# Attention scores of the first 128 queries as three fp32r matmuls of 128 columns, with the FFN weights kept in the raw weight buffers

## What is computed

```
h = _L0_tok_ref(x, log_dt, log_w_real, w_imag, 512)            # (8, 256, 512)
h = h + attn(_layernorm(h), w_q, w_k, w_v, w_o)
h = h + ffn(_layernorm(h), ...)

# attn: 16 query heads, 4 kv heads, head width 128, 256 tokens per image
q, k = q*cos + rotate_half(q)*sin, k*cos + rotate_half(k)*sin
scores = einsum('bhqd,bhkd->bhqk', q, k) / sqrt(128)           # causal, window 256
out = einsum('bhqk,bhkd->bhqd', softmax(scores + bias), v) @ w_o
```

## Time and profile before

| what | value |
|---|---|
| median of 3 runs | 848.62 us (846.26 to 848.85) |
| the profiled execution, its own time | 845.99 us |
| span of the profile | 844.2 us |
| PE busy | 742.8 us, 88% of the span |
| PEld / DVE / ACT / POOL busy | 682.9 / 582.4 / 450.1 / 449.7 us |
| mean granted TensorE clock | 0.968 of full |
| DMA | 26.46 MB in the whole span |

### The profile page before, as it was taken

The page is one execution under the profiler, slowest core; times in us unless marked ns, Lnnn a source line. Parts: engine busy times, 40 slices in busy tenths (PEclk is TensorE's granted clock), DMA queues, the critical chain, the costliest instruction groups (busy, mean ns, idle before and its releaser), DMA issues.

```text
span 844.2 us, 19648 instructions
## 1 busy us (share of the span) xinstructions
PE 742.8 (88%) x6932; PEld 682.9 (81%) x6932; DVE 582.4 (69%) x1618; ACT 450.1 (53%) x1243; POOL 449.7 (53%) x669
## 2 busy tenths in 40 slices
PE   0038748899999999999999999999999999999985
PEld 0027747799999999999999999999999998998772
DVE  7957966677776655565666666566665677777877
ACT  5524415556655756555556565555756645554420
POOL 0198943644454747444547574444746565556522
PEclk9998978899999999999999999999999999999996
DMA  9004370100001102000001020000000000000002
GB/s 199 6 2 89 76 256 25 43 1 1 0 1 38 51 1 76 0 0 0 0 1 50 1 76 0 0 0 1 26 26 1 2 1 26 25 25 25 1 26 75
DMA packets 30533, 26.46 MB, mean 31 GB/s; under 512 B 22476, under 2 KB 22860, under 8 KB 30228
## 3 DMA queue, kind: packets, MB, share of 16 engines
q1 hardware_dynamic: 30484, 25.84, 10.9%
HBM read 17.44 MB, written 8.39 MB: 31 GB/s over the span
## 4 chain that ended last, share of the span: by engine, by line
PE 77%; DVE 11%; POOL 4%; issue 3%; ACT 2%; DMA 1%; DVEq 0%; SPq 0%; ACTq 0%; POOLq 0%
PE bank L1188 17%; PE bank L1190 17%; PE bank L1189 17%; PE bank_pair L1188 4%; PE bank_pair L1190 4%; PE bank_pair L1189 4%; POOL w_lo L421 2%; PE bank L1319 2%; PE bank_pair L1319 2%; DVE bank_pair L878 2%; PE bank_pair L1329 1%; PE bank L1329 1%; PE bank L1333 1%; PE bank L1200 1%; PE bank L1273 1%
## 5 line engine op out<-in xcount | busy, mean ns | idle before, releaser
L1188 PE MATMUL bank<-xt_hi,w_hi 128*128 (+1 forms) x768 | 217.5, 283 | 2.3 <-DVE xt_lo L949 1.5
L1189 PE MATMUL bank<-xt_hi,w_lo 128*128 (+1 forms) x768 | 215.1, 280 | 0.0
L1190 PE MATMUL bank<-xt_lo,w_hi 128*128 (+1 forms) x768 | 215.1, 280 | 0.0
L957 DVE TENSOR_TENSOR kq<-bank,cst 128x512 f32<-128x512 f32 (+1 forms) x96 | 57.9, 603 | 142.0 <-ACT swap L669 106.8
L489 POOL TENSOR_TENSOR swap<-swap,cst 128x512 f32<-128x512 f32 (+1 forms) x96 | 105.7, 1103 | 83.2 <-ACT swap L669 80.0
L1188 PEld LDWEIGHTS bank<-xt_hi,w_hi 128*128 128x128 f32 x768 | 145.2, 189 | 3.3 <-issue 1.9
L1190 PEld LDWEIGHTS bank<-xt_lo,w_hi 128*128 128x128 f32 x768 | 145.0, 189 | 0.0
L1189 PEld LDWEIGHTS bank<-xt_hi,w_lo 128*128 128x128 f32 x768 | 144.8, 188 | 0.0
L347 POOL TENSOR_TENSOR spare<-cst 1x1 f32<-1x1 f32 x87 | 16.6, 191 | 226.1 <-DVE rinv L1091 141.1
L709 ACT ACTIVATE sm<-sm,mx 128x128 f32<-128x128 f32 (+1 forms) x256 | 113.6, 445 | 21.6 <-DVE mx L1081 21.5
L668 ACT ACTIVATE swap<-bank 64x512 f32<-64x512 f32 (+1 forms) x96 | 50.2, 523 | 126.6 <-PE bank L1190 123.8
(11 more groups left out here) (245 smaller groups left out, 1900.3 us busy)
## 6 DMA issues: line engine op xcount, KB each, us to landing
mixed<-st SPq DMA_DIRECT2D x32, 128.0 KB, 2.0
out<-x SPq DMA_DIRECT2D x16, 256.0 KB, 2.1
raw<-in_w_qkv SPq DMA_DIRECT2D x8, 384.0 KB, 3.5
raw<-in_w_o SPq DMA_DIRECT2D x10, 256.0 KB, 2.7
x<-mixed SPq DMA_DIRECT2D x2, 1280.0 KB, 10.3
norm_mem<-in_w_qkv SPq DMA_DIRECT2D x6, 384.0 KB, 3.7
x<-mixed SPq DMA_DIRECT2D x3, 512.0 KB, 5.2
norm_mem<-in_w_o SPq DMA_DIRECT2D x6, 256.0 KB, 2.8
```

The costliest lines, as they stand in the source:

```text
L957: v.tensor_tensor(view(kq), src, table(cosT), ALU.mult).then_inc(kq_cos, 1)
L1188: mmul(dst, lh, rh, start=start and k == 0, stop=False, skip_group_check=True)
L1189: mmul(dst, ll, rh, start=False, stop=False, skip_group_check=True)
L1190: last = mmul(dst, lh, rl, start=False, stop=stop and k == n - 1, skip_group_check=True)
```

## The change

The fp32 matmul of each head's query tile 0 becomes a `split_product` of three fp32r matmuls of 128 columns. For this `kq_hi` and `kq_lo` hold q for all 256 tokens, so that two of the three parts that ACT, POOL (and once DVE) make grow from 128x256 to 128x512. Both tiles get longer. `fw` and `dw` no longer have memory of their own: they become views of `raw`, and SP loads them there once the last raw weights have been split. For the table `pw` the gate weights are loaded near the start into `fw_early`, which lies in memory that the first stage gives back.

```diff
@@ rope_view
     h = slice(2 * j - 1, 2 * j + 1)
-    return (..., (lambda t: t[:, h, P:S]),
-            (lambda t: t[:, j * S:(j + 1) * S].rearrange("p (h q) -> p h q", h=2)))
+    return (..., (lambda t: t[:, h, :]),
+            (lambda t: t[:, (2 * j - 1) * S:(2 * j + 1) * S].rearrange("p (h q) -> p h q", h=2)))
@@ memory
-        fw = sb("fw", [P, KC, FC])
-        dw = sb("dw", [MC, D])
+        spent = raw[:].rearrange("p r c -> p (r c)")
+        fw = spent[:, 0:KC * FC].rearrange("p (k f) -> p k f", k=KC)
+        dw = spent[0:MC, KC * FC:KC * FC + D]
+        fw_early = sb("fw_early", [P, KC, FC], F32, mixer)
-        kh = sb("kq_hi", [P, S + QH * P], F32R)
-        kl = sb("kq_lo", [P, S + QH * P], F32R)
+        kh = sb("kq_hi", [P, (1 + QH) * S], F32R)
+        kl = sb("kq_lo", [P, (1 + QH) * S], F32R)
@@ SP
-            sp.dma_start(fw[:], w_gate).then_inc(gate_in, 16)
-            sp.dma_start(dw[:], w_upd).then_inc(gate_in, 16)
+            sp.dma_start(fw_early[:], w_gate).then_inc(gate_in, 16)
...
             for n in range(KC + 2, NCK * NG):
                 load_raw(n)
+            wait_split(sp, NCK * NG - 1)
+            sp.dma_start(fw, w_gate).then_inc(ffn_in, 16)
+            sp.dma_start(dw, w_upd).then_inc(ffn_in, 16)
             with sp.Fori(0, NB) as bb:
@@ DVE, table pw
-            dve.wait_ge(gate_in, 80)
+            dve.wait_ge(gate_in, 64)
@@ PE, scores
                     bank = banks[3 + j]
-                    mmul(bank[:, 0:P], kq[:, 1 + j, 0:P], kq[:, 0, 0:P], start=True, stop=True, skip_group_check=True)
-                    qs = slice(S + j * P, S + (j + 1) * P)
-                    split_product(bank[:, P:3 * P], [(kh[:, qs], kl[:, qs], kh[:, 0:S], kl[:, 0:S])]).then_inc(s_ready, 1)
+                    for t, cols in ((0, slice(0, P)), (1, slice(P, 3 * P))):
+                        qs = slice((1 + j) * S + t * P, (1 + j) * S + (t + 1) * P)
+                        ks = slice(0, (t + 1) * P)
+                        last = split_product(bank[:, cols], [(kh[:, qs], kl[:, qs], kh[:, ks], kl[:, ks])])
+                    last.then_inc(s_ready, 1)
@@ PE, step, last group
+                        if at == 2:
+                            pe.wait_ge(ffn_in, 32)
                         gate_product(b - 2)
```

More of the change, by code:

```diff
@@ L87, in rope_view @@
     h = slice(2 * j - 1, 2 * j + 1)
-    return ((lambda t: t[:, h, :]), (lambda c: c.unsqueeze(1).to_broadcast([P, 2, S])), (lambda t: t[:, h, P:S]),
-            (lambda t: t[:, j * S:(j + 1) * S].rearrange("p (h q) -> p h q", h=2)))
+    return ((lambda t: t[:, h, :]), (lambda c: c.unsqueeze(1).to_broadcast([P, 2, S])), (lambda t: t[:, h, :]),
+            (lambda t: t[:, (2 * j - 1) * S:(2 * j + 1) * S].rearrange("p (h q) -> p h q", h=2)))
 RUNS = [
@@ L306, in raw_turn @@
             return sum(raw_slot(m) == raw_slot(n) for m in range(n + 1))
-        cst_in, par_in, mix_in, gate_in = sem("cst_in"), sem("par_in"), sem("mix_in"), sem("gate_in")
+        cst_in, par_in, mix_in, gate_in, ffn_in = sem("cst_in"), sem("par_in"), sem("mix_in"), sem("gate_in"), sem("ffn_in")
         raw_in = [sem(f"raw_in{k}") for k in range(6)]
@@ L906, in _ @@
                         sum_b(s, it * 2 + s)
-            dve.wait_ge(gate_in, 80)
+            dve.wait_ge(gate_in, 64)
             for k in range(KC):
-                sel = fw[:, k, 0:NE * SE].rearrange("p (n s) -> p n s", n=NE)
-                mean = fw[:, k, NE * SE:NE * SE + NE]
-                upd = fw[:, k, NE * SE + NE:FC].rearrange("p (n h) -> p n h", n=NE)
+                sel = fw_early[:, k, 0:NE * SE].rearrange("p (n s) -> p n s", n=NE)
+                mean = fw_early[:, k, NE * SE:NE * SE + NE]
+                upd = fw_early[:, k, NE * SE + NE:FC].rearrange("p (n h) -> p n h", n=NE)
                 row = pw[:, k, 0:FC]
@@ L1285, in update_product @@
                 for t in range(TT):
-                    mmul(banks[first_bank + t][:], mt[:, t * P:(t + 1) * P], dw[:], start=True, stop=True).then_inc(d_ready, 1)
+                    mmul(banks[first_bank + t][:], mt[:, t * P:(t + 1) * P], dw, start=True, stop=True).then_inc(d_ready, 1)
             def out_product(i):
```

## The result

| | before | after |
|---|---|---|
| median of 4 runs each, side by side | 848.29 us (846.26 to 848.85) | 856.16 us (856.01 to 856.38) |
| the profiled execution, its own time | 845.99 us | 856.01 us |
| span of the profile | 844.2 us | 854.2 us |

The ratio is 1.0097, 95% interval 1.0080 to 1.0115: slower, as forecast, but by 7.9 us (10.0 between the two profiled executions) where 15.8 were forecast.

What follows compares the result with a forecast made beforehand. PE's unbroken stream was taken to bound the kernel. Scores +13.9, lower clock +0.4, changes of group +1.2 and start +0.3 gave +15.8 us (15.0 to 17.9), so 864 us, range 861 to 867.

Steps and rivals of the forecast that it cites:

- Three short fp32r matmuls for one fp32 product, +13.9 us, and +0.4 at the lower clock: PE's scores: 0.112 us more per head over 124 heads; the first iteration's four heads, at 1.2 GHz, add 0.4.
- x: Price of one 128-column fp32r matmul on PE: taken as 0.112 us, bounded by 0.110 and 0.118.
- The FFN weights ... At nothing: Loading FFN weights into raw after the last split: over 15 us of cover before the first gate product, so no cost.
- POOL's `kq_lo`, +0.84 an iteration: POOL's subtractions: two of three parts grow from 0.85 to 1.27 us each; covered in ordinary iterations.
- The changes of group, +1.2 us: At three changes of group w_lo, queued behind kq_lo on POOL, makes PE wait 0.39 us longer each.
- Waits for `w_lo` from 0.8 to 2.0 us: Sign to look for: PE's total wait for POOL's w_lo rises from 0.8 to 2.0 us.
- Ordinary POOL and ACT at nothing: In ordinary iterations POOL's longer kq_lo has 3.2 us of cover; ACT's longer roundings follow an unchanged first part: no cost.
- This too is covered: In FFN iterations POOL sat idle 1.65 us behind kq_lo, so its longer kq_lo costs nothing.
- The last scores at nothing, the start +0.3: Last scores' extra 0.45 us hides behind DVE's ot_lo; at the start PE waits 0.27 longer for DVE's kq_lo.
- The sum of +15.8: All terms together over the whole kernel: +15.8 us, range 15.0 to 17.9.
- the rivals' formula: Whole change's cost for any x, used to price the rivals: 112 x (3x − 0.224) + 2.8 us.
- loads half hidden: Rival: weight loads partly hidden behind short matmuls, x from 0.075 to 0.105, about 0.090; +8 us, 856; 4 in 100.

Runs made afterwards that it cites:

- e17: The whole change, with an unused gap of 128 bytes ahead of xt_hi so it stands as before within 256 bytes; 863.80 us, ratio 1.0199.
- e13: The whole change, but in iteration 6 of a group DVE makes its w_lo share behind both output additions, not between them; 856.86 us, ratio 1.0109.
- e3: The kernel after the change, with query tile 0 of all four heads one fp32 matmul again; 847.43 us, ratio 0.9998.
- e6: The kernel before, with only fw and dw allocated behind all other tiles, so xt_hi lies 4224 bytes lower; 840.42 us, ratio 0.9912.
- e11: The kernel before, with an unused gap of 128 bytes ahead of xt_hi; 840.30 us, ratio 0.9897.
- e9: The kernel before, with fw and dw allocated ahead of x, so w_hi lies 4224 bytes higher and xt_hi stays; 839.37 us, ratio 0.9900.
- e7: The kernel before, with dbs (128 bytes) allocated behind all others, so xt_hi and the tiles behind lie 128 bytes lower; 841.12 us, ratio 0.9918.
- e10: The kernel before, with an unused gap of 256 bytes ahead of xt_hi; 847.42 us, ratio 0.9988.

## Why the prediction was right or wrong, point by point

- **Three short fp32r matmuls for one fp32 product, +13.9 us, and +0.4 at the lower clock: right.** An ordinary `scores` went from 2.31 to 2.74 us, +0.43 where 0.45 was forecast. x is 0.111 (0.685 less the 0.353 of three long ones, by three), between the low bound of 0.110 and the 0.112 taken. That the load of 128 weight columns paces a short matmul fits the loads of L1209, 0.10 to 0.11 apart with two moving columns; no run varied the load alone. The first iteration's `scores` went from 4.43 to 5.26 us, +0.83 where 0.85 was forecast. The 81 ns that the Trainium skill ("TensorE: Matmul & The Clock Gate", "Back-to-back issue gap") would have given were not reached in fp32r, nor does any row show a faster load.
- **"The FFN weights ... At nothing": here the prediction failed.** As transfers they do cost nothing: issued at 660.6 us, read at 686.1, no wait. But with their memory went 4224 bytes from in front of `xt_hi`, and the forecast gave the diff's memory part no term and no bound. It was worth 7.6 us (863.80 of e17 less 856.16; 7.2 between their profiled executions), almost the whole gap between 15.8 forecast and 7.9 measured.
- **POOL's `kq_lo`, +0.84 an iteration: mis-sized.** The total over 93 parts rose from 78 to 113 us, +1.13 an iteration. The part of 128x512 was priced well (1.27 forecast, 1.285 measured). The error was the 0.85 for a part of 128x256, a mean over unequal ones: the first takes about 1.05 to 1.15 beside DVE and stays, the two that grow take 0.737 each.
- **The changes of group, +1.2 us: mis-sized, and under another name.** Against two ordinary iterations of the same kernel, iterations 6 and 7 stand 0.48, 0.81 and 0.80 us longer before and 1.14, 1.47 and 1.48 in e17: +0.67 each, 2.0 in all, since POOL's `w_lo` comes 1.1 later and not 0.84 (1.1 less 0.43 of PE's own is the 0.67, as 0.84 less 0.45 was the 0.39). "Waits for `w_lo` from 0.8 to 2.0 us" was wrong on its face, 3.4 for `x` and none for `w_lo`; e13 shows both.
- **Ordinary POOL and ACT at nothing: right between 190 and 650 us, wrong with the FFN.** "This too is covered" stood on 1.65 us of POOL idle. In e17 an FFN iteration grew 0.58 us, 0.15 more than its scores. In e3, with fp32 scores, it is 25.0 us against 24.6 in e6, and putting the short matmuls in only makes it 25.08: the scores alone no longer set the length there. What grew on DVE is one tiny instruction beside the longer `kq_lo`. Its groups before, and then after:

```profile
L1044 DVE TENSOR_TENSOR norm<-norm x6: 176/176/179, 689.2 to 814.0; 128x16 f32<-128x16 f32 x6
```

```profile
L1048 DVE TENSOR_TENSOR norm<-norm x6: 179/723/726, 697.1 to 824.0; 128x16 f32<-128x16 f32 x6
```

  In one iteration after the change, beside POOL's `kq_lo`:

```profile
721.58 1.29 POOL L497 TENSOR_TENSOR kq_lo<-kq,kq_hi 128x512 fp32r<-128x512 f32 x1
722.18 0.72 DVE L1048 TENSOR_TENSOR norm<-norm 128x16 f32<-128x16 f32 x1
```

  It ends at 722.90, just behind POOL's 722.87. Its 0.55 us more, less 0.14 by which the instruction at the head of the same chain got shorter (L1041, 0.31 before; L1045, 0.17 after), makes 0.4, the size of what e3 has over e6. That this one instruction is the cause is worked out, not shown: no run took it away, and the trace records no wait of PE there.
- **The last scores at nothing, the start +0.3: right** (+0.1 from the last scores on, +0.2 to the first).
- **The sum of +15.8: met at equal places of the tiles (+16.1 between medians), in part by luck, and wrong for the kernel as it is.** Of e17's 17.2 us between profiled executions the first iteration has 1.7, where 0.85 was forecast, the three changes of group have 2.0 beyond the scores, where 1.2 was forecast, and the five FFN iterations 0.7, where nothing was; iterations 1 to 5 grew by 1.6 in place of 2.2. Also, the rivals' formula, 112 x (3x − 0.224) + 2.8, gives 15.3 at x = 0.112 and not 15.8: it left out the four heads of the first iteration. That moves no case by more than half a microsecond. The rival "loads half hidden" names 856 too, but by x = 0.090, which the heads' 0.685 us rule out: the right time for a wrong reason.

The cost of the rest of the edit, the longer `kq` parts above all, is also seen alone: e3 less e6 is 7.0 us between medians, 4.5 between their profiled executions (844.91 and 840.42), far over the 1.5 that the sum gave them. Of the 4.5, the changes of group have 2.7, the FFN iterations 1.8 and the part behind the last scores 0.9, whose cause stays open; the first six iterations give 0.8 back.

## What to carry to other kernels

When an edit frees or adds memory, list which tiles move and by how much before pricing its instructions, and compare the starts of matmuls it does not touch: here 128 bytes were worth 7 us, half of the edit's own cost. In a kernel bound by fp32r matmuls small gaps ahead of the moving operand are a cheap thing to try, each with a measurement: of the gaps of 64, 128, 192 and 256 bytes only that of 128 helped, and two made it slower. e11, the kernel before with 128 unused bytes, takes 840.30 us and e9 839.37, and both beat the kernels before and after. Replacing an fp32 product of 128 columns by three fp32r ones costs half as much again here (0.33 us for 0.224), since each of the three starts 0.11 us behind the last. Whether it pays with more columns, no run here shows.

## What the runs showed of the hardware that was not expected

- An unbroken stream of fp32r matmuls of 256 columns, each with a load of 128, starts every 113.3, 117.8, 118.7 or 119.9 ns, by the distance of moving and loaded operand modulo 256 bytes and by how the stream was entered. The Trainium skill, page "SBUF — State Buffer", says in section "SBUF: two separate sides" that PE never waits on anyone, and lists its two read ports as independent in section "Who interferes with whom". The pace measured here isn't independent of where the two operands lie: nothing but places in memory was changed in e6, e7, e9 and e11, and PE's pace changed by 4%. Why, no run shows.
- A DVE instruction of 128x16 took 723 ns beside a POOL subtraction and 176 without. One of 128x768 took 1210 ns when it began 0.4 us ahead of the end of a POOL subtraction and 2109 when it began 1.3 ahead, and POOL's next subtraction took 2.55 us in place of 1.84 both times. The Trainium skill, page "SBUF — State Buffer", section "Who interferes with whom", says that a DVE instruction with two inputs in SBUF contends with a POOL instruction that reads SBUF; section "SBUF: two separate sides" says that whichever starts first holds the shared ports for its whole instruction. The trace agrees: both DVE instructions end behind POOL's, the small one 0.03 us and the large one 0.8.
- Most of the spread of 5 us between executions of the kernel before (845.57 to 850.77) may lie ahead of the first scores: in the profiles of the eighteen kernels these begin between 140.0 and 143.4 us, and the kernel e10, whose profiled execution took 850.4 against a median of 847.42, has 143.4. No run tested it.
